# Batch 1's folded values are centred by rows; in groups 5 to 7 VectorE scales and adds in one instruction

## The reference

```python
x = L0_attn_query
x = x + _layernorm(_L0_attn_ref(_layernorm(x), ...))
x = x + _layernorm(_L0_ffn_ref(_layernorm(x), ...))

# in _L0_ffn_ref, its last step: 16 heads, 16 slots o of each batch
out = _mha(x, o, o, c_Wq, c_bq, c_Wk, c_bk, c_Wv, c_bv, c_Wo, c_bo)

def _layernorm(x, axis=-1, eps=1e-05):
    m = jnp.mean(x, axis=axis, keepdims=True)
    v = jnp.var(x, axis=axis, keepdims=True)
    return (x - m) / jnp.sqrt(v + eps)
```

## Time and profile before

| what | value |
|---|---|
| median of three runs | 487.43 us |
| the profiled execution | 487.64 us |
| its span | 485.9 us |
| TensorE (PE) busy | 403.1 us, 83% |
| VectorE (DVE) busy | 310.0 us, 64% |
| ScalarE (ACT) busy | 232.1 us, 48% |
| GpSimd (POOL) busy | 151.9 us, 31% |

### The profile page before, as it was taken

The page is one execution under the profiler, slowest core; times in us unless marked ns, Lnnn a source line. Parts: engine busy times, 40 slices in busy tenths (PEclk is TensorE's granted clock), DMA queues, the critical chain, the costliest instruction groups (busy, mean ns, idle before and its releaser), DMA issues. The chain is left out here.

```text
span 485.9 us, 6975 instructions
## 1 busy us (share of the span) xinstructions
PE 403.1 (83%) x2091; PEld 248.2 (51%) x2091; DVE 310.0 (64%) x1177; ACT 232.1 (48%) x424; POOL 151.9 (31%) x251
## 2 busy tenths in 40 slices
PE   3886566779888987997879999999998679999981
PEld 3542223235444554665646775634443237888870
DVE  3599999969999987586214236233332124979984
ACT  2226647747686795778444734100000001355765
POOL 3105645454858522432201110010000000344453
PEclk9997888788999998999998999999997879999997
DMA  4294011011010229367219667749999999601223
GB/s 145 88 300 127 8 44 43 1 43 38 8 43 2 76 88 309 117 217 275 103 56 316 246 215 262 261 181 395 395 391 396 392 377 368 221 1 45 86 88 129
DMA packets 44030, 83.78 MB, mean 172 GB/s; under 512 B 1878, under 2 KB 36316, under 8 KB 39388
## 3 DMA queue, kind: packets, MB, share of 16 engines
q1 hardware_dynamic: 42936, 82.15, 48.0%
q10 hardware_dynamic: 1060, 1.22, 0.8%
HBM read 70.78 MB, written 12.58 MB: 172 GB/s over the span
## 5 line engine op out<-in xcount | busy, mean ns | idle before, releaser
L1063 PE MATMUL bank<-Wz,yT 128*128 128x512 f32 x128 | 71.0, 707 | 25.9 <-DVE top L1640 23.2
L1063 PEld LDWEIGHTS bank<-Wz,yT 128*128 128x128 f32 x128 | 28.1, 228 | 61.6 <-issue 48.1
L1640 DVE MAX8 top<-bank 128x8 f32<-128x32 f32 x512 | 51.5, 181 | 1.9 <-ACT arena L736 1.7
L997 ACT ACTIVATE d<-d 128x32 f32<-128x32 f32 x16 | 3.7, 229 | 90.6 <-DVE d L2020 90.6
L576 POOL TENSOR_SCALAR veps<-mv 128x4 f32<-128x4 f32 x24 | 6.0, 248 | 107.0 <-DVE mv L1568 75.3
L684 POOL TENSOR_TENSOR work<-work 128x512 f32<-128x512 f32 x16 | 16.6, 1061 | 66.2 <-DVE work L2085 66.2
L1096 PE MATMUL bank<-aWo,hoT 128*128 128x256 f32 x128 | 36.0, 404 | 0.1
L715 ACT ACTIVATE arena<-arena,shift,rstd 128x256 f32<-128x256 f32 x64 | 33.2, 594 | 3.7 <-POOL shift L699 2.9
L1130 PE MATMUL bank<-arena,Wd 128*128 128x512 f32 x64 | 29.2, 598 | 3.2 <-ACT arena L799 3.2
L1159 PE MATMUL bank<-d,work 128*128 128x256 f32 x128 | 30.3, 382 | 0.9 <-ACT d L827 0.9
L1501 PE MATMUL bank<-scr,work 128*128 128x256 f32 x128 | 29.1, 381 | 1.6 <-ACT work L1010 1.6
(11 more groups left out here) (262 smaller groups left out, 879.0 us busy)
## 6 DMA issues: line engine op xcount, KB each, us to landing
arena<-in_L_ffn_e_W_dram SPq DMA_DIRECT2D x10, 1024.0 KB, 7.8
x<-in_L_ffn_e_W_dram SPq DMA_DIRECT2D x9, 1024.0 KB, 9.2
arena<-in_L_ffn_e_Wg_dram SPq DMA_DIRECT2D x7, 1024.0 KB, 11.2
scr<-in_L_ffn_e_W_dram SPq DMA_DIRECT2D x7, 1024.0 KB, 13.7
work<-in_L_ffn_e_W_dram SPq DMA_DIRECT2D x5, 1024.0 KB, 13.7
xin<-in_L_attn_query_dram SPq DMA_DIRECT2D x8, 512.0 KB, 4.1
x<-in_L_attn_query_dram SPq DMA_DIRECT2D x1, 4096.0 KB, 16.6
out_dram<-x SPq DMA_DIRECT2D x8, 512.0 KB, 5.6
```

Of the source, the lines that this page charges most:

```text
L1063: mm = pe.matmul(bZ[t % 2][:, :], yT[:, c, t * P:(t + 1) * P], Wz[:, c, :], start=(c == 0), stop=(c == C - 1))
L1640: mx = v.max(top[:, h * TG + t, :], bZ[t % 2][:, h * NS:(h + 1) * NS])
```

## The change

The values of batch 1 are centred: from each row of Vc[1] the mean over its 256 outputs is subtracted, on VectorE, after total(1) (centre_values: one reduction, one scaling, two subtractions). A token's output is a sum of such rows, so its own mean is then zero, and the norm needs no shift. For portions of groups 5 to 7 (LONE = 5) GpSimd computes only variance plus epsilon and the power; ScalarE does nothing; VectorE multiplies each tile by rstd and adds the stream in one scalar_tensor_tensor for each tile, twelve in all. Group 4 is centred too, but is scaled and added as before. On VectorE the order behind the loop becomes norm_out(6), scale_and_add(5), scale_and_add(6), norm_out(7), norm_out(8), scale_and_add(7), scale_and_add(8). TensorE waits for the centring before the scores of group 4.

```diff
@@ out_roots, GpSimd
-                if k >= 3:
+                if k >= LONE + 3:
+                    hold(c_out, k - 2)
+                elif k >= 3:
                     hold(c_norm, tiles_by(k - 3))
                 pool.tensor_scalar(veps[:, w, lo:hi], mv[:, w, lo:hi, 1], EPS, None, ALU.add).then_inc(c_vare, 1)
+                if j >= LONE:
+
+                    pool.wait_ge(c_vare, k + LONE + 1)
+                    pool.tensor_tensor(rstd[:, w, lo:hi], veps[:, w, lo:hi], mhalf[:, lo:hi], ALU.pow).then_inc(c_root, 1)
+                    return
@@ ScalarE
-                if j >= 2:
+                if 2 <= j < LONE + 2:
                     apply_out(j - 2)
                 put_out(j)
-            for k in range(NG - 2, len(portions)):
-                apply_out(k)
@@ TensorE, at j + 2 == GB
                     pe.wait_ge(dve_part, CS + 6)
+                    pe.wait_ge(centred, 4)
@@ VectorE
+            def centre_values():
+
+                v.wait_ge(dve_part, CS + 6)
+                v.tensor_reduce(vmean, Vc[:, 1, :, :], AX_X, ALU.add).then_inc(centred, 1)
+                v.wait_ge(centred, 1)
+                v.tensor_scalar(vmean, vmean, 1.0 / D, None, ALU.mult).then_inc(centred, 1)
+                v.wait_ge(centred, 2)
+                for m in range(2):
+                    v.tensor_scalar(Vc[:, 1, m, :], Vc[:, 1, m, :], vmean[:, m:m + 1], None, ALU.subtract).then_inc(centred, 1)
@@ norm_out, VectorE
-                    v.wait_ge(c_rst, k - 2)
+                    v.wait_ge(c_rst if k < LONE + 3 else c_root, k - 2)
@@ VectorE
+            def scale_and_add(k):
+                j, lo, hi = portions[k]
+                v.wait_ge(back[j % 2], 16 * (j // 2 + 1))
+                v.wait_ge(c_root, k + 1)
+                for t in range(lo, hi):
+                    o_ = v.scalar_tensor_tensor(out=co[j % CO][:, t, :], in0=co[j % CO][:, t, :], scalar=rstd[:, k % 3, t:t + 1],
+                                                in1=x[:, j * TG + t, :], op0=ALU.mult, op1=ALU.add)
+                o_.then_inc(c_out, 1)
@@ VectorE, the order
                 total(j, j % 2)
+                if j == 1:
+                    centre_values()
...
             norm_out(NG - 2)
-            add_stream(NG - 3)
+            scale_and_add(NG - 3)
+            scale_and_add(NG - 2)
             norm_out(NG - 1)
             norm_out(NG)
-            for k in range(NG - 2, len(portions)):
-                add_stream(k)
+            for k in range(NG - 1, len(portions)):
+                scale_and_add(k)
```

More of the change, by code:

```diff
@@ L216, in build @@
         crs = work[:, 7296:7360]
+        vmean = work[:, 7360:7362]
         xs = A['L0_attn_query'].rearrange("b (p j) d -> p b j d", p=P)
@@ L320, in build @@
         c_norm = sem("c_norm")
+        centred = sem("centred")
         c_out = sem("c_out")
@@ L338, in build @@
         CS = PREP + 2 * MS
+        LONE = NG - 3
         def tiles_by(k):
```

## The result

In the first comparison the changed kernel took 483.03 us (median of four runs, 482.59 to 485.12) against 487.47 us before (486.13 to 487.61): ratio 0.9921, interval 0.9897 to 0.9944. (A ratio is an estimate from all runs of its comparison with its 95% interval; it is not exactly the quotient of the two medians, which is 0.9909 here.) Two more comparisons of the same pair of kernels gave 0.9959 (0.9944 to 0.9975) and 0.9950 (0.9932 to 0.9969). Over all of them the changed kernel's median is 484.44 us (28 runs) and that of before 487.00 us (72 runs): **2.56 us less**; without the first comparison it is 2.5 us. Two executions of the kernel before that took 2128 us are left out of every number here.

The account below looks back on a forecast made before the run. TensorE was taken to bound the last stage until about 475.4 us, then a serial tail of hand-overs. Centring at 0 and a tail 2.35 us shorter, against a median of 487.43 us, gave 485.1 us, range 483.9 to 486.6 us.

Parts of the forecast that it names:

- (b): GpSimd's root(6) beside VectorE's scaling of group 5, partly held by it: done at 474.7 us (bounds 474.28 and 475.6).
- (c): VectorE's scale-and-add of group 6: four instructions in 1.35 us, ending at 476.13 us.
- (d): Group 7's statistics, queued behind group 6's scaling: start 476.25 us against 476.06 before, nothing lost or won.
- (e): GpSimd's power for group 7's first half, without shift: 2.34 us after the statistics start, at 478.59 us.
- (f): VectorE's scaling of group 7's first half: 478.67 to 479.40 us.
- (g): GpSimd's second root for group 7, held beside the first half's scaling: done at 480.12 us (bounds 479.7 and 480.4).
- (h): VectorE's last scale-and-add, after 0.08 + 0.73 us: ends at 480.93 us.
- Part 1: Centring batch 1's values on VectorE after total(1): 1.7 to 2.3 us, under 2.5 us of cover, costed at 0.
- Part 2: Tail of groups 5 to 7: twelve VectorE scale-and-adds of 0.42 us, no shift or ScalarE scaling; 2.35 us less.
- Rival C: Scale-and-add far slower in the tail: at 0.80 us start to start, 489.1 us; chance 0.04, shared with centring that shows.
- A: Blocking both ways in the tail: GpSimd's power holds VectorE for 1.04 us; 1.3 us less, 486.2 us; chance 0.11.
- B: GpSimd kept out through a whole row of VectorE scalings in the tail; kernel at 486.2 us; chance 0.13.

Follow-up runs that it names:

- group7_only: The changed kernel with the new path for group 7 alone, groups 5 and 6 handled as before the change; median 485.62 us, ratio 0.9979 to the kernel before.
- after_more: The changed kernel run a third time with no edit; median 484.39 us, ratio 0.9950 to the kernel before.
- squares: The changed kernel with group 7's VectorE statistics replaced by ScalarE's summed squares, scale-and-add reading PSUM; median 482.56 us, ratio 0.9921 to the kernel before.

## Why the prediction was right and wrong

The measured times are those of the first profile after, less 0.16 us for the later begin of the stage:

| step | predicted | measured |
|---|---|---|
| (a) scaling of group 5 | 472.85 to 474.20 | 472.69 to 474.33 |
| (b) root(6) done | 474.7 | 474.44 |
| (c) scaling of group 6 ends | 476.13 | 476.21 |
| (d) statistics of group 7 start | 476.25 | 476.13 |
| (e) power of the first half done | 478.59 | 478.45 |
| (f) scaling of the first half ends | 479.40 | 479.44 |
| (g) power of the second half done | 480.12 | 479.62 |
| (h) last VectorE instruction ends | 480.93 | 480.60 |
| (i) from there to the span's end | 2.61 | 2.64 |

**The bounding by TensorE** was right: its steps stayed 7.78 us apart. **Part 1** was right: 1.98 us between 1.7 and 2.3, hidden, the scaling of 128x2 held back to 0.67 us until GpSimd's weighing ended at 423.10 us. What was not foreseen is the pause of 0.45 us, worth 0.07 us.

**Part 2, the price of the instruction**, was too low: 0.48 us with 0.40 us from start to start, not 0.42 and 0.31. Four took 1.64 to 1.67 us instead of 1.35, two 0.88 instead of 0.73, 0.9 us more over the four rows of scalings. The spacing was taken from the statistics, which have one tensor input; whether that makes the difference no run shows. A spacing of 0.40 us lies inside the forecast's own bounds of 0.27 to 0.42 us. **The collision of step (b) and (g)** was too dear: I held each of GpSimd's two instructions to the end of a scaling; the first steps took 0.23 and 0.22 us, the powers 1.12 and 0.87 us instead of 1.04 and 0.71.

The errors partly cancel, but not as those 0.9 us suggest. Group 5's scaling and the first half's run beside a root of GpSimd that ends later (474.44 against 474.33 us, 479.62 against 479.44), so their price is not on the path. Along the path, by the table, the measured times gained 0.26 us on the forecast at (b), lost 0.34 at (c), gained 0.20 at (d), where the statistics began 0.08 us before the scaling had ended and not 0.12 us behind it, gained 0.02 at (e) and 0.36 at (g), and lost 0.17 at (h): 0.33 us in all. The sum was 2.35, the stage gave 2.66 us (76.97 - 74.31). Rival C needed 0.66 us from start to start. The rule of the Trainium skill, SBUF — State Buffer, section "SBUF: two separate sides", that the one which comes second fully blocks, fits the wide addition of group7_only and the held scaling of the centring, but the trace does not agree with it for a running power: four scalings beside one took 1.64 us, and 1.67 us beside none.

**The step that failed** is the last one of the numbers, the range: "0.3 to 0.4 us of spread on either side", from three runs of 486.13 to 487.61 us. The runs of this kernel spread over 483.3 to 489.0 us with a standard deviation of 1.1 us (72 runs). Four of these runs and four of the 28 of the changed kernel, drawn at random, give a difference of medians with a standard deviation of 0.7 us, twice the allowance. The prediction gave "a median off by the spread of the runs" a chance of 0.02. The first medians were 0.5 us above and 1.4 us below those of many runs, 487.00 and 484.44 us. The change is worth 2.56 us by these; the forecast's 2.35 us, taken from 487.00 us, give 484.65 us, 0.2 us from the measured median. The direction, and a change of over 0.3%, came out as forecast.

That the first result was a mere draw is likely and not shown. A difference of 4.4 us or more comes in about one of 100 such draws; three of the first four changed runs lie below 483.3 us, and one of the 24 later ones. Two of the three have the highest mean clock of all 28 changed runs, 0.958, and the one later run with that clock is the low one (482.80 us); but the third has 0.940, where the seven later runs took 483.58 to 485.78 us. None of the three was profiled: the first profile is of the slowest of the four. What speaks against a larger effect of the change is that two larger comparisons didn't repeat it, and that the profiled low run of after_more has the same last stage.

The chances hold a gap too: A and B fall just short of "faster", so 0.81 for it is 0.11 more than the forecast's 0.70, and nothing says from where.

A second part of the reasoning was wrong in its reading, if not in its number: step (d) called groups 5 and 6 neutral. The statistics of group 7 did start no earlier, but group7_only shows 0.70 us there, as the addition of group 6 stood in the way of group 7's scaling and root. The times of (f) and (g) had that addition gone without saying so.

## What to carry to other kernels

Measure a stage against its own begin: here a change of 0.5% repeated to a few hundredths of a microsecond from profile to profile, while the difference of two medians of four runs was off by three quarters of it. Behind the last TensorE work this kernel's end was a sum of hand-overs, so look for the engine that can be left out of the row (here ScalarE's scaling by one instruction, then VectorE's statistics by ScalarE's squares, 2.7 and 2.1 us) and for wide instructions that stand in front of the last narrow ones. A property made once on the weights, here rows with mean zero, costs 2 us under cover and makes several steps for each token unnecessary.

## What the runs showed of the hardware

- A scalar_tensor_tensor of 128x256 with a scale for each partition took 479 ns with 0.39 to 0.40 us from start to start, from SBUF or, in squares, from PSUM (476 ns), where a two-input operation of the same size took 422 ns.
- GpSimd's first step took 0.97 us beside a VectorE addition of 1024 elements (group7_only) and 0.23 or 0.24 us beside a row of 256-wide instructions.
- A running power of GpSimd did not hold VectorE: four 256-wide scalings took 1.64 us beside one and 1.67 us beside none. The power itself was stretched by 0.08 to 0.16 us.
- A tensor_scalar of 128x2 from SBUF took 0.67 instead of 0.17 us beside GpSimd's multiplication; the reduction of 512 elements in front of it was not held, 0.63 us.
- An accumulating activation is two instructions, 0.38 us for 256 elements from PSUM and 0.20 us for reading the sum, which overlap: two pairs took 0.84 us.
- Executions of the kernel before differed by up to 5.3 us in one comparison (483.33 to 488.66 us), with TensorE's granted clock dipping at other places in the two profiles compared.
